# A transformer layer on one core: routing five of eight batches to their experts through a sorted DRAM table

## The reference, cut to what matters

```python
h = onehot(x) @ embeddings                                  # x: 8 x 256 token ids, D = 256
h = h + attention(layernorm(h), w_qkv, w_proj)              # 16 heads of 16, rotary positions, softmax
y = layernorm(h)
scores = einsum('bsh,eh->bse', y, gate_w)                   # 8 experts
chosen = argmax(scores, axis=-1)
expert_out = einsum('bsh,efh->bsef', y, expert_w)           # expert_w: 8 x 256 x 256
h = h + (y + einsum('bsef,bse->bsf', expert_out, onehot(chosen)))
```

## Time and profile before

| | |
|---|---|
| Median of 3 runs | 321.82 us (321.7 to 324.18) |
| The profiled execution, its own time | 324.0 us |
| Its span, first to last instruction | 322.2 us |
| TensorE busy | 280.8 us, 87% |
| VectorE busy | 243.8 us, 76% |
| ScalarE busy | 127.0 us, 39% |
| GpSimd busy | 85.7 us, 27% |
| Mean granted clock of TensorE | 0.944 of full speed |

### The profile page before, as it was taken

The page is one execution under the profiler, slowest core; times in us unless marked ns, Lnnn a source line. Parts: engine busy times, 40 slices in busy tenths (PEclk is TensorE's granted clock), DMA queues, the critical chain, the costliest instruction groups (busy, mean ns, idle before and its releaser), DMA issues.

```text
span 322.2 us, 5465 instructions
## 1 busy us (share of the span) xinstructions
PE 280.8 (87%) x2000; PEld 201.1 (62%) x2000; DVE 243.8 (76%) x595; ACT 127.0 (39%) x261; POOL 85.7 (27%) x96
## 2 busy tenths in 40 slices
PE   0388489888878999989998999999999999999894
PEld 0267367454655777667765776676766766667582
DVE  6766667667798879887997799687988974657663
ACT  3032213643766543345343444353535435330100
POOL 4743500013567402250234113400210210210301
PEclk9999775558999999999999999999999999999998
DMA  4269492480191084015600470039000000001000
GB/s 115 73 247 149 66 161 28 83 119 1 25 161 27 9 142 58 4 36 113 91 6 32 92 117 4 0 94 139 4 33 4 1 28 10 3 1 35 0 33 33
DMA packets 11590, 19.14 MB, mean 59 GB/s; under 512 B 2012, under 2 KB 4903, under 8 KB 11436
## 3 DMA queue, kind: packets, MB, share of 16 engines
q1 hardware_dynamic: 10776, 18.23, 30.4%
q0 software_dynamic: 768, 0.55, 0.7%
q10 hardware_dynamic: 20, 0.02, 0.0%
HBM read 5.30 MB, written 2.10 MB: 23 GB/s over the span
## 4 chain that ended last, share of the span: by engine, by line
PE 47%; DVE 26%; issue 11%; POOL 5%; DMA 4%; ACT 4%; SPq 1%; POOLq 0%; DVEq 0%; ACTq 0%
PE e_bank L422 13%; PE o_bank L552 7%; DVE neg_max L863 7%; PE f_bank L422 7%; DVE acc L942 5%; PE t_pair L517 5%; DMA stacks<-parts 3%; PE s_pair L488 3%; POOL qk L342 2%; PE s_pair L422 2%; PE m_bank L564 2%; PE m_bank L422 2%; POOL res L360 2%; PE o_bank L422 1%; ACT parts L695 1%
## 5 line engine op out<-in xcount | busy, mean ns | idle before, releaser
L731 ACT ACTIVATE probs<-t_pair 128x512 f32<-128x512 f32 x128 | 69.7, 596 | 91.4 <-PE t_pair L517 91.0
L863 DVE TENSOR_REDUCE neg_max<-s_pair 128x2 f32<-128x512 f32 x128 | 82.0, 684 | 15.0 <-PE s_pair L488 15.0
L488 PE MATMUL s_pair<-stacks 48*128 48x256 f32 x256 | 54.8, 341 | 5.8 <-DVE neg_max L863 2.8
L517 PE MATMUL t_pair<-stacks 50*128 50x256 f32 x256 | 50.0, 325 | 2.0 <-DVE neg_max L863 1.7
L517 PEld LDWEIGHTS t_pair<-stacks 50*128 50x128 f32 x256 | 35.5, 199 | 24.4 <-issue 21.4
L422 PE MATMUL e_bank<-ew_h,y_h 128*128 128x512 f32 x92 | 40.3, 439 | 4.6 <-DVE acc L938 2.7
L488 PEld LDWEIGHTS s_pair<-stacks 48*128 48x128 f32 x256 | 38.9, 209 | 8.8 <-DVE neg_max L863 5.0
L552 PE MATMUL o_bank<-probs,vals 128*32 128x256 f32 x512 | 36.4, 405 | 1.2 <-ACT max_rows L695 1.2
L942 DVE SCALAR_TENSOR_TENSOR acc<-e_bank,mask,acc 128x256 f32<-128x256 f32 x66 | 28.9, 479 | 11.2 <-PE e_bank L422 11.2
L422 PE MATMUL e_bank<-ew_h,y_l 128*128 128x512 f32 x92 | 36.3, 395 | 0.0
L422 PE MATMUL e_bank<-ew_l,y_h 128*128 128x512 f32 x92 | 36.3, 395 | 0.0
(11 more groups left out here) (132 smaller groups left out, 532.1 us busy)
## 6 DMA issues: line engine op xcount, KB each, us to landing
stacks<-parts SPq DMA_DIRECT2D x48, 256.0 KB, 7.0
ew_raw<-in_expert_w SPq DMA_DIRECT2D x1, 2048.0 KB, 8.2
out<-res SPq DMA_DIRECT2D x8, 256.0 KB, 2.1
probs<-in_w_qkv SPq DMA_DIRECT2D x2, 384.0 KB, 3.8
stacks<-max_rows SPq DMA_DIRECT2D x30, 8.0 KB
h<-in_emb,ids POOLq DMA_INDIRECT x16, 2.6
probs<-in_w_proj SPq DMA_DIRECT2D x1, 256.0 KB, 2.6
stacks<-ones SPq DMA_DIRECT2D x6, 16.0 KB
```

Source lines behind the costliest of these rows:

```text
L488: m = mm(s_pair[:, half, t * N:(t + 1) * N], stacks[b % STACKS][r:r + KS, pair, 0, t * P:(t + 1) * P], stacks[b % STACKS][r:r + KS, pair, ...
L517: m = mm(t_pair[:, half, c * N:(c + 1) * N], stacks[b % STACKS][r:r + KM, pair, 1, c * P:(c + 1) * P], stacks[b % STACKS][r:r + KM, pair, ...
L731: nc.scalar.activation(probs[:, (2 * v + half) % RING, :, :].rearrange("p c n -> p (c n)"), t_pair[:, half, :], ACT.Exp, scale=SCALE).then ...
L863: v.tensor_reduce(neg_max[:, k // 4, :, 4 * half + k % 4], s_pair[:, half, :].rearrange("p (t n) -> p t n", t=NT), AX.X, ALU.max, negate=T ...
```

## The change

Batches 0 to 4 (`ROUTED = 5`) no longer run the dense experts. Their normed rows are written into a DRAM table ordered by expert, read back as 17 blocks of 128 rows that all belong to one expert, multiplied by that expert's weights alone, written to a second table, and gathered back by token. Batches 5 to 7 keep the dense experts, and their steps.

In the order of time:

- At the start, GpSimd makes a triangle of ones, VectorE copies it and a square of ones (`upper`, `every`). The constants come in one longer table.
- The weight parts `ew_h`, `ew_l` are made in steps 2 to 5, two units in each (slots 4 and 10), not in step 1.
- In steps 2 to 6, for each routed batch (`place_at`: slot 6 of the step after `choose`; for batch 4 slot 13 of step 5): `count_places` (two matmuls with the mask), `find_rows` (8 VectorE instructions: the table row of each token), `send_rows` (two indirect DMAs from GpSimd). Batch 4's post stage uses a table `QUICK` that ends at slot 12.
- Behind batch 4's `find_rows`: `plan_blocks`, 18 VectorE instructions in a chain, which find the first row and the expert of each block; eight blank tiles (four from GpSimd, four from SyncE), then on SyncE a register load and a DMA for each block (`fetch`).
- In steps 6 and 7, a pair of blocks in every second slot from slot 4 of step 6: `turn_blocks` (a register load for each block, a wait for its DMA, four transposes), `block_high` (ScalarE), `block_low` (VectorE), `block_products` (12 matmuls of 256 columns, the weights found through the register), `block_result` (ScalarE), `store_blocks` (SyncE). Six pairs fall into step 6, two pairs and a single block into step 7.
- From slot 11 of step 7: `bring_back` (ten indirect gathers on GpSimd), `add_back` (five sums on GpSimd), `store_routed`.
- The maxima of batches 2 to 6 use `e_bank` instead of `o_bank`, and those of batches 3 to 6 go at slot 9 instead of 11. The dense experts of batch 5 use `s_pair` alone. `base` is kept in `h0`; `yn` has two buffers; third stack, `rope_a`, `qk` and `xn` lend their memory when they are done.

The diff, cut to its core:

```diff
+ROUTED = 5
+BLOCKS = ROUTED * 2 + N_EXP - 1
+PAIRS = (BLOCKS + 1) // 2
+REGION = (ROUTED * 2 + 1) * P
...
+        QUICK = dict(POST, o_low=6, proj=7, residual=8, stats=8, g_norm=9, y=10, y_low=10, gate=11, gate_t=12, choose=12)
...
-            return 9 if b < 3 else 11
+            return 9 if b <= ROUTED + 1 else 11
+        def place_at(b):
+            return SLOTS * (b + 1) + 13 if b == ROUTED - 1 else SLOTS * (b + 2) + 6
+        def turn_at(m):
+            return SLOTS * (ROUTED + 1) + 4 + 2 * m
+        def product_at(m):
+            return turn_at(m) + 1
+        def return_at(b):
+            return SLOTS * (ROUTED + 2) + 11 + 2 * b
...
-            return [e_bank, f_bank] + s_bank if b >= NB - 3 else [e_bank]
+            return s_bank + [e_bank, f_bank] if b > ROUTED else s_bank
...
+            def fetch(js):
+                for j in js:
+                    if j == 0:
+                        sp.wait_ge(plan_ok, PLAN)
+                        wait(sp, t_ps, ROUTED * NH + NH)
+                        sp.wait_ge(blanks_out, 16 * N_EXP // 2)
+                        sp.wait_ge(more_blanks_out, 16 * N_EXP // 2)
+                        for i in range(2):
+                            sp.wait_ge(rows_out[i], 16 * NT * ((ROUTED + 1 - i) // 2))
+                    row = sp.value_load(block_row[0:1, j:j + 1], min_val=0, max_val=N_EXP * REGION - P)
+                    sp.dma_start(slot(j), sorted_rows[bass.ds(row, P), :]).then_inc(block_in[j], 16)
...
                 if b >= 0 and here(b, 1):
+                    if b == ROUTED + 1:
+                        fetch(range(5, 10))
+                        store_blocks(range(2))
                     maximum(b + 1, 0)
-                if here(b, -2):
+                if b == ROUTED:
+                    send_blanks()
+                    fetch(range(5))
+                if b == ROUTED + 1:
+                    fetch(range(10, BLOCKS))
+                    store_blocks(range(2, 5))
+                if b == ROUTED + 2:
+                    store_blocks(range(5, PAIRS))
+                if here(b, -2) and not routed(b - 2):
                     store(b - 2)
...
+            def bring_back(b):
+                if b == 0:
+                    pool.wait_ge(out_at_ok, 1)
+                    pool.wait_ge(blocks_out, 16 * BLOCKS)
+                for j in range(b * NT, (b + 1) * NT):
+                    g.indirect_dma_start(ring[:, j, :], None, sorted_out,
+                                         bass.IndirectOffsetOnAxis(ap=out_at[:, j:j + 1], axis=0),
+                                         bounds_check=BLOCKS * P - 1, oob_is_err=False).then_inc(returned[b], 16)
...
-                    if s % 2 and b == 1:
-                        expert_weights([s // 2])
+                    if 2 <= b < 6 and s in (4, 10):
+                        expert_weights([2 * (b - 2) + (s == 10)])
...
+            def turn_blocks(m):
+
+                if m == 0:
+                    pe.wait_ge(plan_ok, PLAN)
+                    wait(pe, v_ok, NB)
+                for j in blocks_of(m):
+                    columns[j] = pe.value_load(block_column[0:1, j:j + 1], min_val=0, max_val=(N_EXP - 1) * D)
+                    pe.wait_ge(block_in[j], 16)
+                wait(pe, bl_ok, m)
+                for j in blocks_of(m):
+                    for c in range(C):
+                        k = (j % 2 * C + c) * P
+                        i = tr(f_bank[:, k:k + P], slot(j)[:, c * P:(c + 1) * P], ident[:, :])
+                i.then_inc(bt_ps, 1)
...
+                for j in blocks_of(m):
+                    w = columns.pop(j)
+                    i = product(e_bank[:, j % 2 * D:(j % 2 + 1) * D],
+                                lambda c: pair_parts(0, m)[:, (j % 2 * C + c) * P:(j % 2 * C + c + 1) * P],
+                                lambda c: pair_parts(1, m)[:, (j % 2 * C + c) * P:(j % 2 * C + c + 1) * P],
+                                lambda c: ew_h[:, c, bass.ds(w, D)], lambda c: ew_l[:, c, bass.ds(w, D)])
+                i.then_inc(block_ps, 1)
...
-                    if here(b, -2) and unit_in(b, s) is not None:
+                    for k in range(ROUTED):
+                        if g_at == place_at(k):
+                            count_places(k)
+                    for m in range(PAIRS):
+                        if g_at == turn_at(m):
+                            turn_blocks(m)
+                    for m in range(PAIRS):
+                        if g_at == product_at(m):
+                            block_products(m)
+                    if here(b, -2) and not routed(b - 2) and unit_in(b, s) is not None:
                         experts(b - 2, p, unit_in(b, s), expert_banks(b - 2))
```

More of the change, by code:

```diff
@@ L967, in step @@
                     for k in batches(post, "stats", g_at):
[L968 removed]
+                        if not tight(k):
                             g_norm_a(k)
@@ L998, in step @@
                         choose(k, k % 2)
+                    for k in range(ROUTED):
+                        if g_at == place_at(k):
+                            find_rows(k)
+                            if k == ROUTED - 1:
+                                plan_blocks()
+                    if b == ROUTED + 1 and s == 8:
+                        plan_return()
+                    for m in range(PAIRS):
+                        if g_at == turn_at(m):
+                            block_low(m)
             dve.sem_inc(acc_ok, 1)
```

347 lines of the change are left out of this document (296 added, 51 removed).

## The result

The changed kernel takes 350.9 us (median of 4 runs, 345.8 to 354.9), the kernel before 323.0 us in the same comparison: a ratio of 1.078, interval 1.062 to 1.093. The forecast was 309.8 us, in 297 to 321. It is slower, and the range does not hold it. The profiled execution (351.4 us) has a span of 349.7 us, 27.5 more than before. Some runs of a kernel are slow as a whole, the profiled one of the change among them, so ratios, and differences between the times of two kernels, are taken here from the medians of the fast runs alone: 348.1 us for the change, 298.5 in experiment 1, 318.0 in 13 and 339.1 in 17.

The account below looks back on a forecast made before the run. TensorE was taken to bound most steps before, VectorE steps 2 to 4 after. Terms 0.4 - 1.0 - 25.9 - 2.4 + 8.3 + 7.9 + 0.7 = -12.0 us gave 312.0 us profiled, median 309.8 us, range 297 to 321.

Parts of the forecast that it names:

- Steps 2 to 4, dense experts gone: Attention steps without dense experts: 24.7 us each, VectorE the bound, 25.9 us saved over three steps.
- so 9.4 us for a step: 33.5 - 9.4 = 24.1 us.: Saving per step, scaled from 7.03 us between six-visit pieces of steps 1 and 3 to eight units.
- given back: Steps 2 to 4: 1.1 us a step deducted for VectorE waiting beside GpSimd's weight subtractions in the measured piece.
- `find_rows` costs its 1.7 us: Steps 2 to 4: eight small VectorE instructions add 1.7 us a step; the count products on TensorE cost nothing.
- Step 5: Step with `find_rows` twice and the plan: 25.1 us of VectorE at 92% gives 27.3 us, 2.4 us saved.
- Step 6: Twelve blocks replace the dense experts: 12 us of pairs, 7.8 of register loads, 1.7 of clock; 36.0 us, +8.3 us.
- 27.63 - 13.18: Step 6: its time before, less TensorE's dense expert work, the base to which the block terms were added.
- The end: Step 8 and after: ten gathers and five sums, 17 us on GpSimd, just fit before `g_rs`; +0.7 us, bounds 0 to 4.
- C: Rival: register loads on TensorE's queue and SyncE's are dear, 2.1 us each instead of 1.0; 328.5 us, chance 0.10.
- B: Rival: register loads on TensorE's queue are hidden and the clock holds, 12.4 us less; 297.4 us, chance 0.24.
- D: Rival: GpSimd holds VectorE's small `find_rows` and plan instructions, ten holds of 1.1 us; 320.8 us, chance 0.10.
- E: Rival: TensorE's clock falls to half in steps 2 to 4, 3 x 11.3 us more; 344 us, chance 0.04.

Follow-up runs that it names:

- experiment 1: Changed kernel with every call of the routing taken out, batches 0 to 4 stored without their experts; 302.1 us (324.0 before).
- 13: Changed kernel without the blocks' transposes, parts, products and result copies, each fetched block stored as it came; 319.3 us, ratio 0.985.
- 17: Changed kernel with the counts of batches 0 to 3 on TensorE in slot 4 instead of 6; 339.5 us, ratio 1.049.
- 15: Changed kernel without any routing, and with the expert weights' conversions back in step 1; 296.0 us, ratio 0.921.
- 14: Changed kernel with only the counts and `find_rows` of the routing, `find_rows` reading a table instead of waiting for the counts; 302.1 us, ratio 0.940.
- 2: Changed kernel with only `count_places` and `find_rows` left of the routing; 304.7 us, ratio 0.945.
- 9: Changed kernel with only counts and `find_rows` of the routing, plus 14 unread matmuls behind each count of batches 0 to 3; 306.4 us, ratio 0.947.
- 10: Changed kernel with unread matmuls in TensorE's pauses: behind counts, at the plan, and ahead of block 0; 347.5 us, ratio 1.078.
- 6: Changed kernel without register loads on TensorE, every block multiplied by expert 0's weights at a fixed address; 349.3 us, ratio 1.088.
- 3: Changed kernel with the products of a pair of blocks two slots behind its transposes instead of one; 339.4 us, ratio 1.048.
- 12: Changed kernel with the next pair's high part ahead of the previous pair's result copies on ScalarE; 344.6 us, ratio 1.067.
- 4: Changed kernel without the gathers by token and the five sums on GpSimd; 346.4 us, ratio 1.071.
- 8: Changed kernel with `plan_blocks` moved behind VectorE's maxima of slot 15 of step 5; 349.7 us, ratio 1.087.
- 5: Changed kernel with `find_rows` and `send_rows` of batches 0 to 3 one slot later, behind that slot's maxima; 350.4 us, ratio 1.084.
- 16: Changed kernel with products two slots behind the transposes, high part ahead of the result copies, and weight conversions back in step 1; 338.1 us, ratio 1.045.
- 7: Changed kernel with products two slots behind the transposes, `find_rows` a slot later, and gathers of batches 3 and 4 later in step 8; 342.4 us, ratio 1.059.
- 18: Changed kernel with counts two slots earlier, products two slots behind the transposes, and high part ahead of the result copies; 331.4 us, ratio 1.024.

## Why the prediction was wrong

The step that failed first is the term "Steps 2 to 4, dense experts gone", and in it two assumptions.

- *"so 9.4 us for a step: 33.5 - 9.4 = 24.1 us."* Two pieces of the same visits are only comparable if the same work stands in both. The v projection and four transposes did not, and I scaled the error by 8/6. Measured by leaving the experts out: 6.2 us a step (27.3), 18 us for three instead of 28. The 1.1 us "given back" for the moved weight subtractions went the wrong way too: one of the two in a step fell on `yn`, 1.6 us instead of 0.7 (1, 15; in the change in steps 2 and 3).
- *VectorE bounds, so `find_rows` costs its 1.7 us.* It costs nothing as work (14) and 3.1 us as a meeting (2, 14, 17). I listed the counts on TensorE as free, "beside VectorE's work", and did not ask what stood ahead of them in TensorE's queue while VectorE waits. Some 1 us of the 3.1 may be the clock, by the price of a dip in 14 and 15; the filled pauses (9, 10) give no more than that.
- *Step 5*, +5.4 us: without routing it takes 26.4 us, with counts 28.8, and with the plan 32.7. That is 3.9 us more for the plan, as long as it is itself, and less than forecast. What was short is the 25.1 us of VectorE "at 92%": VectorE had 24.1 us and filled 74% of the step, while TensorE stood 4.9 us at the plan and the granted clock was 0.80.
- *Step 6.* The block terms, 12 us of matmuls, 7.8 of loads, 5.0 and 2.9 in step 7, make 27.7 us; the blocks measure 30 (13). The size was nearly right and the mechanism wrong: no register load shows (6), and in place of the loads' 10.7 us stand the waits between transposes and products (9.3 us in the trace; 3 and 12 take them away in whole or in part) and the late first block (2.96 us, "which the sum puts at nothing"; the fetch itself, its load, issue and landing, was left out of it). I wrote that "VectorE and ScalarE stay under that", which is true of their sums and says nothing of their order. The 9.6 us that step 6 is longer than forecast lie in the other part, *27.63 - 13.18*: it takes all of TensorE's 13.2 us off the step, which makes 14.5 us. The step without the blocks' work measures 27.2 us (13), and with the counts alone still 20.0 us at a clock of 0.90 (2).
- *The end*, 0.7 us: some 2 to 3 us (4), with bounds of 0 and 4. The gathers hold GpSimd 21.7 us, not 17. They began in their slot, 11 of step 7, but this slot came late: `g_rs` of batch 6 stood at 300.3, 26 us behind batch 7's first exponential, instead of 15, and GpSimd had waited 39 us for it.
- *Rivals.* C was the slower side, with the wrong mechanism: it decides from 1.7 us a load, and a load with its register instructions is about 0.7 on SyncE. B, loads hidden, was right on the loads alone. D is not seen in the small instructions, which take 0.15 to 0.32 us in the change, about as assumed; it is seen in `yn`. E was half right: the clock did fall in steps 2 to 4, for 3.4 us in each. It held in 1 and 17 with TensorE busy for 82% of the same steps, so the smaller share alone does not bring it down, and in the change it followed a pause of 2 us. But it fell in 9, 10 and 15 as well, in steps in which TensorE never stood idle for 1 us. What decides it stays open.

What held: the price of the blocks in its size, the plan's length, and the signs that were named for a failure (a step of 30 us, TensorE's wait for a block's DMA, the gathers right ahead of `g_rs`). The slower outcome had a chance of 0.14, through C and E, and came at neither's price. The way from the kernel without routing to the change is: 298.5 us without routing (1); 6.2 more for the counts (2); 13.3 more for the scatters, the plan, the blanks, fetches, stores and gathers (13), 2 to 3 of them the gathers (4); and 30.1 more for the work on the blocks: 348.1. How the remaining 10 us of the 13.3 divide between the plan's pause, the fetch's lateness and the clock was not separated; 8 shows only that moving the plan moves the cost.

## What to carry to other kernels

- When an engine's work is taken out, the next bound need not be another engine's sum: here it was a chain between two engines that are each busy 82 to 84%. Measure the pace by leaving the work out, and if a piece of the old trace must stand in for it, list the instructions of both pieces before dividing.
- A cheap pair of instructions on two engines costs what the later one's queue holds ahead of it. Issue the producer well before the consumer: two slots of distance were worth 9 us of 348 here (17); moving the consumer instead was worth nothing (5).
- In a hand-written slot schedule, keep a full slot of other work between the ends of a chain with three handovers (transpose, copy, subtract, multiply): 10 us here (3). On the engine in the middle, put the handover ahead of the copies nobody waits for: 3.5 us (12). The two took away the same wait, so together they were worth no more than the first (16).

## What was not expected of the hardware

- In the change the granted clock fell in step after step behind a single pause of TensorE of about 2 us, and came back 3.4 us later (6.8 in 2); with the pause gone it held at full speed with TensorE busy for 82% of 82 us (17). A pause is not needed for it, though: in steps 3 and 4 of 15 and 9, and in step 3 of 10, it fell with no idle stretch of TensorE as long as 1 us.
- Once down near the end of step 5 it stayed at half for 10 to 34 us in the forms of this kernel (34.1 in 7, 27.3 in 18, 13.7 in the change and, without any routing, in 1). What sets this length was not found. The runs of the change spread over 9 us (345.8 to 354.9), and single differences of 2 or 3 us between forms are not to be read.
- A register load on TensorE's queue ahead of a wait cost nothing that could be measured (6). On SyncE, in front of a DMA, it is about 0.7 us with its register instructions, the load alone 0.27 us.
- A `tensor_scalar` of VectorE (two of 128x256) took 1.59 us beside a sum of GpSimd and 0.73 us without it (1, 15).
